# A two-layer graph network: the adjacency's own pipeline moved eight steps forward, its last row block by DMA transposes

## What is computed

```python
q, k, v = x @ Wq.T + bq, x @ Wk.T + bk, x @ Wv.T + bv
a = q @ k.T / sqrt(D) + adj + adj            # 4096 x 4096
x1 = layernorm(x + softmax(a) @ v)
h = relu(adj @ (x1 @ W1) + b1)               # y = x1 @ W1
out = layernorm(x1 + adj @ (h @ W2) + b2)
```

## Time and profile before

| | |
|---|---|
| median of 3 runs | 1905.79 us |
| the profiled execution, whole | 1905.41 us |
| its span, first to last instruction | 1903.6 us |
| TensorE busy | 1896.3 us |
| VectorE busy | 1085.0 us |
| ScalarE busy | 861.9 us |
| POOL busy | 115.9 us |
| DMA, mean over the span | 244 GB/s |
| chain that ended last | TensorE 99% |

### The profile page before, as it was taken

How to read it: one execution, slowest core, us unless ns; L and a number is a source line. 1 busy time by engine, 2 the same in 40 slices (tenths; PEclk the granted TensorE clock), 3 DMA queues, 4 the chain that set the end, 5 groups by cost and what they waited for, 6 DMA issues and landing times.

```text
span 1903.6 us, 26546 instructions
## 1 busy us (share of the span) xinstructions
PE 1896.3 (100%) x9265; PEld 889.0 (47%) x9265; DVE 1085.0 (57%) x2107; ACT 861.9 (45%) x1848; POOL 115.9 (6%) x211
## 2 busy tenths in 40 slices
PE   9999999999999999999999999999999999999998
PEld 4444444444444444444444444444444454444446
DVE  7787666666666666666666666666666620001334
ACT  6655554555555555555555555455545611010112
POOL 0000000000000000000000000000000000002334
PEclk9999999999999999999999999999999999999999
DMA  8664599999999999999999999999999999989996
GB/s 253 164 140 113 134 232 230 225 231 225 223 225 227 225 230 232 222 229 220 230 228 226 228 226 226 229 223 225 228 218 240 215 354 387 387 301 360 394 394 243
DMA packets 801015, 463.73 MB, mean 244 GB/s; under 512 B 646768, under 2 KB 654704, under 8 KB 800880
## 3 DMA queue, kind: packets, MB, share of 16 engines
q1 hardware_dynamic: 792816, 448.03, 93.7%
q10 hardware_dynamic: 8064, 14.00, 2.0%
HBM read 220.99 MB, written 92.01 MB: 164 GB/s over the span
## 4 chain that ended last, share of the span: by engine, by line
PE 99%; DMA 0%; issue 0%; DVE 0%; ACT 0%; SPq 0%; POOL 0%; POOLq 0%; ACTq 0%
PE bank L597 15%; PE bank L599 15%; PE bank L598 15%; PE bank L719 12%; PE bank L721 12%; PE bank L720 12%; PE bank L842 5%; PE bank L844 5%; PE bank L843 5%; PE bank L625 1%; PE bank L806 0%; PE bank L802 0%; PE bank L803 0%; PE bank L863 0%; PE bank L865 0%; PE bank L864 0%
## 5 line engine op out<-in xcount | busy, mean ns | idle before, releaser
L1013 ACT ACTIVATE tsp<-ring,sc 128x512 f16<-128x512 f32 x248 | 179.0, 722 | 599.0 <-DMA tsp<-tsp 598.3
L1399 DVE SCALAR_TENSOR_TENSOR ring<-bank,sc,adj_in 128x512 f32<-128x512 f32 x256 | 192.2, 751 | 398.2 <-PE bank L599 392.9
L597 PE MATMUL bank<-xT,gT 128*128 128x512 f16 x1024 | 388.1, 379 | 0.0
L598 PE MATMUL bank<-xT,gT 128*128 128x512 f16 x1024 | 388.1, 379 | 0.0
L599 PE MATMUL bank<-xT,gT 128*128 128x512 f16 x1024 | 388.1, 379 | 0.0
L719 PE MATMUL bank<-xv,tsp 128*128 128x512 f16 x1008 | 382.0, 379 | 0.1
L720 PE MATMUL bank<-xv,tsp 128*128 128x512 f16 x1008 | 382.0, 379 | 0.0
L721 PE MATMUL bank<-xv,tsp 128*128 128x512 f16 x1008 | 382.0, 379 | 0.0
L1214 DVE SCALAR_TENSOR_TENSOR tsp<-adj_in,s_a,tsp 128x512 f16<-128x512 f32 x248 | 184.7, 745 | 46.3 <-ACT tsp L1021 45.8
L1214 DVE SCALAR_TENSOR_TENSOR tsp<-ring,sc,tsp 128x512 f16<-128x512 f32 x248 | 184.9, 746 | 0.1
L1001 ACT ACTIVATE ring<-ring,bias 128x512 f32<-128x512 f32 x256 | 181.0, 707 | 8.8 <-DVE bias L1416 8.8
(11 more groups left out here) (270 smaller groups left out, 2173.3 us busy)
## 6 DMA issues: line engine op xcount, KB each, us to landing
adj_in<-in_adj SPq DMA_DIRECT2D x256, 256.0 KB, 3.2
at_dram<-tsp SPq DMA_DIRECT2D x248, 256.0 KB, 3.2
xv<-at_dram SPq DMA_DIRECT2D x54, 1024.0 KB, 14.4
adj_in<-at_dram SPq DMA_DIRECT2D x29, 1024.0 KB, 14.4
xT<-at_dram SPq DMA_DIRECT2D x20, 1024.0 KB, 14.0
xv<-in_x SPq DMA_DIRECT2D x8, 1024.0 KB, 10.0
g_dram<-tsp SPq DMA_DIRECT2D x32, 256.0 KB, 4.0
gT<-g_dram SPq DMA_DIRECT2D x32, 256.0 KB, 3.6
```

Of the source, the lines that this page charges most:

```text
L597: pe.matmul(dst, ah, bh, start=first, stop=False)
L598: pe.matmul(dst, ah, bl, start=False, stop=False)
L1013: act.activation(p_split(e)[:, 0:BANK], p, ACT.Copy, scale=col[f"p_up{batch(TW * kb)}"]).then_inc(a_p, 1)
L1399: dve.scalar_tensor_tensor(t, s_bank[s % S_BANKS][:, :], col[f"k_l{batch(s // KB)}{batch(TW * (s % KB))}"], adj_in[:, s % AR, :], ALU.mult ...
```

## The change

The adjacency's own pipeline gets its own step number. adj_plan gives for each score step s the adjacency steps that are made in it: at first v = s; in eight steps from s = 19 on, each seven after the last, two of them; from then on v = s + 8. SP, ScalarE, VectorE and POOL run load_adj, absolute_sums, adj_sum, the all-reduce, adj_scale, adj_hi, adj_lo, transpose_adj and store_at by v. So the last row block's adjacency goes through the same DMA transposes and stores as all others and is in at_dram when the scores end. TensorE's adj_transposes and the conversions after them go. The first eight units are loaded whole, 1 MB each, in an order of their own: units 0 to 3 stand between the transposes of blocks 250 to 254, units 8 and 9 stand ahead of 6 and 7. T(e) stands below for the transposes of score block e (transpose_p). Left out below are the hunks that drop the names at_bank, p_adj, the call of adj_transposes and last_adj_lo, and that call adj_plan.

```diff
@@ -88,7 +88,7 @@
 O_AT = (4, 7, 10, 13)
 STATS_DELAY, NORM_DELAY, STORE_DELAY = 1, 5, 6
 Y_LAST = (11, 14)
-ADJ_AT = (1, 2, 4, 5, 7, 8, 10, 11)
+ADJ_EARLY, ADJ_FROM = 8, 2 * KB
 Y_DRAM = NT - 4


@@ -107,6 +107,19 @@


     return list(range(t + XG + 2, t + 2 * XG + 2)) if t % XG == XG - 2 and t < NT - XG - 2 else []
+
+
+def adj_plan():
+
+
+    plan, early = [], 0
+    for s in range(NS + 2 * KB):
+        steps = [s + early]
+        if s >= ADJ_FROM and early < ADJ_EARLY and (s + early) % KB == STATS_AT - 1:
+            early += 1
+            steps.append(s + early)
+        plan.append(steps)
+    return plan


 def unit_plan():
...
@@ -472,19 +485,18 @@
                 else:
                     sp.wait_ge(p_pv, NS)
                     for i in range(2):
-                        sp.wait_ge(d_ast[i], 16 * TAIL // 2)
-                last = TAIL - KB + kb
+                        sp.wait_ge(d_ast[i], 16 * NS // 2)
+                last = TAIL + kb
                 sp.wait_ge(d_ast[last % 2], 16 * (last // 2 + 1))
-                sp.dma_start(slots[kb][:, 0:TW - 1, :, :].rearrange("p r b n -> p r (b n)"), units_dram[LAST, kb][:, 0:TW - 1, :]
-                             ).then_inc(d_unit[kb], 16)
+                sp.dma_start(slots[kb].rearrange("p r b n -> p r (b n)"), units_dram[LAST, kb]).then_inc(d_unit[kb], 16)

             def load_unit(l):
                 ic, kb, slot, after = loads[l]
                 if after:
                     sp.wait_ge(p_unit, after)
                 elif slot < KB + 3:
-                    sp.wait_ge(p_adj, min(3 + 4 * (slot - KB), KB))
-                    sp.wait_ge(v_al, TAIL)
+                    sp.wait_ge(v_add, NS)
+                    sp.wait_ge(v_al, NS)
                     if slot == KB + 2:
                         sp.wait_ge(p_pv, NS)
                 else:
@@ -516,23 +528,23 @@
                     transpose_p(TAIL - 1)
                     transpose_x1(NT - 3)
                     transpose_p(TAIL)
-                a = s - ADJ_LAG
-                if 0 < a <= NS:
-                    store_at(a - 1)
-                if 0 <= a < TAIL:
-                    transpose_adj(a)
                 if s == 4:
                     store_g(NT // XG - 1)
                     for q in (10, 11):
                         load_adj(q)
-                if 9 < s + AHEAD < NS and s + AHEAD >= 12:
-                    q = s + AHEAD
-                    if q == AR - 1:
-                        sp.wait_ge(a_w1, 1)
-                        sp.wait_ge(v_w1, 1)
-                    if q >= AR:
-                        sp.wait_ge(v_al, q - AR + 1)
-                    load_adj(q)
+                for v in adj_steps[s]:
+                    a, q = v - ADJ_LAG, v + AHEAD
+                    if 0 < a <= NS:
+                        store_at(a - 1)
+                    if 0 <= a < NS:
+                        transpose_adj(a)
+                    if 12 <= q < NS:
+                        if q == AR - 1:
+                            sp.wait_ge(a_w1, 1)
+                            sp.wait_ge(v_w1, 1)
+                        if q >= AR:
+                            sp.wait_ge(v_al, q - AR + 1)
+                        load_adj(q)
                 if NS - Y_EARLY <= s + 1 < NS:
                     load_y(s + 1 - (NS - Y_EARLY))
                 if kb == GT_AT and 1 <= r < NT - 1:
@@ -550,24 +562,23 @@
                         sp.wait_ge(v_y, j + 1)
                         sp.dma_start(y_dram[j], y_st[:, j % 2, :, :].rearrange("p two f -> p (two f)")).then_inc(d_y[j % 2], 16)

-            for i in range(KB):
-                if i:
-                    transpose_p(TAIL + i)
-                if i == 1:
-                    store_at(TAIL - 1)
-                if i == 3:
-                    load_first_unit(0)
-                if i == 5:
-                    store_x1(NT - 2)
-            load_first_unit(1)
-            load_first_unit(2)
+            transpose_p(TAIL + 1)
+            store_at(NS - 1)
+            for i in range(2, 6):
+                transpose_p(TAIL + i)
+                load_first_unit(i - 2)
+            store_x1(NT - 2)
+            for i in range(6, KB):
+                transpose_p(TAIL + i)
+            load_first_unit(4)
             sp.wait_ge(p_x1, 1)
             sp.wait_ge(d_x1, 16 * (NT - 1))
             sp.dma_start(xr[:, :], x[P * (NT - 1):P * NT, :]).then_inc(d_xr, 16)
-            for kb in range(3, KB):
-                load_first_unit(kb)
+            load_first_unit(5)
             for l in range(KB, KB + 2):
                 load_unit(l)
+            for kb in range(6, KB):
+                load_first_unit(kb)
             store_x1(NT - 1)

             sp.dma_start(w2_s, w2[:, :]).then_inc(d_late, 16)
@@ -756,17 +767,6 @@
                     last = pe.transpose(ht_bank[c % 2][:, P * j:P * (j + 1)], hs[c % 2][:, P * j:P * (j + 1)], ident)
                 last.then_inc(p_h, 1)

-            def adj_transposes(kb):
-                if kb == 0:
-                    pe.wait_ge(g_id, 4)
-                    pe.wait_ge(v_add, NS)
-                if kb >= 2:
-                    pe.wait_ge(v_al, TAIL + kb - 1)
-                for j in range(TW):
-                    last = pe.transpose(at_bank[kb % 2][:, P * j:P * (j + 1)],
-                                        adj_in[:, (TAIL + kb) % AR, P * j:P * (j + 1)], ident)
-                last.then_inc(p_adj, 1)
-
             for s in range(NS + LAG):
                 r, kb = divmod(s, KB)
                 if s < NS:
...
@@ -822,8 +820,6 @@
                 slot = loads[load][2]
                 if half == 0:
                     pe.wait_ge(d_unit[slot], 16 * (sum(1 for l in loads[:load + 1] if l[2] == slot) + (slot < Y_DRAM // TW)))
-                    if n == 0:
-                        pe.wait_ge(v_al, TAIL + kb + 1)
                     if conv == 1 and k == 0:
                         pe.wait_ge(a_h, i + 1)
                         pe.wait_ge(v_h, i + 1)
@@ -1020,15 +1016,6 @@
                     act.wait_ge(d_at[a % 2], 16 * (a // 2))
                 act.activation(asp[a % 2][:, 0:BANK], adj_in[:, a % AR, :], ACT.Copy, scale=s_a[:, r:r + 1]).then_inc(a_ah, 1)

-            def last_adj_hi(kb):
-                if kb == 0:
-                    act.wait_ge(v_sa, NT)
-                act.wait_ge(p_adj, kb + 1)
-                if kb == 6:
-                    act.wait_ge(v_al, TAIL)
-                act.activation(slots[kb][:, TW - 1, 0:TW, :], at_bank[kb % 2][:, :].rearrange("p (b n) -> p b n", n=P), ACT.Copy,
-                               scale=s_a[:, NT - 1:NT]).then_inc(a_ah, 1)
-
             def x1_hi(r):
                 act.wait_ge(v_x1, r + 1)
                 if r >= 1:
@@ -1062,25 +1049,20 @@
                 e = s - EXP_LAG
                 if 0 <= e < NS:
                     exponentials(e)
-                if s + 1 < NS:
-                    absolute_sums(s + 1)
-                a = s - ADJ_LAG
-                if 0 <= a < TAIL:
-                    adj_hi(a)
+                for v in adj_steps[s]:
+                    if v + 1 < NS:
+                        absolute_sums(v + 1)
+                    if 0 <= v - ADJ_LAG < NS:
+                        adj_hi(v - ADJ_LAG)
                 if s >= 2 * KB and kb == X1_AT:
                     x1_hi(r - 2)
                 if s >= 3 * KB and kb == YOUT_AT:
                     y_hi(r - 3)
             for i in range(KB):
                 exponentials(TAIL + i)
-                if i % 2:
-                    last_adj_hi(i // 2)
-                if i == 3:
+                if i == 6:
                     y_hi(NT - 3)
-                if i == 7:
-                    last_x1_hi(NT - 2)
-            for kb in range(KB // 2, KB):
-                last_adj_hi(kb)
+            last_x1_hi(NT - 2)
             y_hi(NT - 2)
             last_x1_hi(NT - 1)

...
@@ -1496,12 +1473,13 @@
                     row_max(s)
                     if kb == KB - 1:
                         exp_bias(r)
-                        adj_sum(r)
-                if kb == 0 and 1 <= r <= NT:
-                    adj_scale(r - 1)
-                a = s - ADJ_LAG
-                if 0 <= a < TAIL:
-                    adj_lo(a)
+                for v in adj_steps[s]:
+                    if v % KB == KB - 1 and v < NS:
+                        adj_sum(v // KB)
+                    if v % KB == 0 and KB <= v <= NS:
+                        adj_scale(v // KB - 1)
+                    if 0 <= v - ADJ_LAG < NS:
+                        adj_lo(v - ADJ_LAG)
                 if s >= 2 * KB:
                     if kb == STATS_AT:
                         attention_rows(r - 2)
@@ -1514,17 +1492,13 @@
             p_lo(TAIL - 1)
             for i in range(KB):
                 p_lo(TAIL + i)
-                if i % 2:
-                    last_adj_lo(i // 2)
-                if i == 3:
+                if i == 4:
                     attention_rows(NT - 2)
+                if i == 5:
```

(23 more changed lines are left out.)

6 lines of the change are left out of this document (removed).

## The result

The changed kernel takes 1925.14 us (median of four runs, 1922.41 to 1926.85) where the kernel before takes 1905.68: 1.0101 times as long, interval 1.0083 to 1.0118. It is slower by 19.5 us. The prediction was 1909.3, in a range up to 1912.3. The profiled execution took 1925.05 us, with a span of 1923.2 against 1903.6.

A forecast was written before the change was run, and what follows sets the result against it. TensorE's own instruction list was taken as the bound. Handover waits of 5.9 less 3.5 removed gave +2.5, plus 0.9 for a pause, rounded to +3.5 on the median 1905.79: 1909.3 us, range 1904.9 to 1912.3.

The forecast's parts named there:

- the score stage: Eight double adjacency steps, score steps 19 to 68: SP's lateness is recovered from its waits; cost nothing, bounds 0 and +2 us.
- Rival D: Score stage: double steps hold up TensorE, 2 us over the forecast, 1911.3 us; chance 0.06.
- The removed work: Eight groups of 4 TensorE transposes between 1508.6 and 1539.8 us go, all on the path: -3.5 us.
- The handover: From 1505 to 1540 us, transposes wait behind units: waits 5.9, gain 3.5, +2.5 us; with the pause +3.5.
- the pause: Handover: the DMA queue stands nearly still among the new loads; bounds 0 and 1.7 us, 0.9 taken.
- A: Handover: units don't hold up the transposes, so the unit stream decides, -0.3 to +1.4, about 1906.3 us; chance 0.22.
- C: Handover: every turn from a transpose to a unit costs extra, +6.1, 1911.9 us; chance 0.22.
- B: The whole gain arrives, 1902.3 us, if the queue finds the 2 to 4 us it lacks; chance 0.06.
- The unit stream: Second stage: last unit lands 2.2 to 3.9 us later with 2.5 to spare; -0.3 to +1.4 us without handover waits.

The follow-up runs named there:

- e1: Changed kernel with its eight double steps 15 or more score steps apart instead of 7; 1912.63 us, 1.0040 times the kernel before.
- e10: Changed kernel with its eight double steps still 7 apart, but from step 163 on instead of step 19; 1927.21 us, 1.0113 times the kernel before.
- e2: Changed kernel with ScalarE doing the adjacency's sums and high half ahead of the exponentials in each step; 1918.98 us, 1.0069 times the kernel before.
- e3: Changed kernel with the loads of units 0 to 3 behind the last transposes instead of between them; 1920.64 us, 1.0078 times the kernel before.
- e4: Changed kernel with the edits of e2 and e3 together; 1913.56 us, 1.0041 times the kernel before.
- e6: Changed kernel with the edits of e1 and e3 together; 1909.56 us, 1.0022 times the kernel before.
- e7: e1 with the first eight units loaded without their fourth row block (0.75 MB), leaving part of a product wrong; 1909.91 us, 1.0024 times the kernel before.
- e5: e1 with the first two units issued at score steps 251 and 253, the rest behind later transposes; 1907.43 us, 1.0011 times the kernel before.

## Why the prediction was wrong

**The step that failed: the score stage, costed at nothing with a bound of +2; it was +13.0.** The double step's own lateness was right (3.6 to 4.5 forecast, 4.7 measured for block 10), and so was SP's order of work. The next sentence was wrong: SP's waits, 152 us in 1240, were taken as time that a late SP gets back, 4.5 us in seven steps. It got back 1.6 (4.7 to 3.1 and 6.3 to 4.7). The free time was overrated too: the prediction had 4.6 us at worst, while block 46 in the kernel before landed at 460.17 and was used at 463.63, 3.5 us later. The waits are not idle time with a deadline behind it. They end when VectorE has done the work of a step that itself began with a landing of SP's own transposes, or when SP's own transposes land (3.1 us at least). Move SP by 4 us and the end of these waits moves too. e1 shows the accumulation, e10 that only the spacing counts, e2 that the loop through ScalarE is about half of it; for the other half, the landings of SP's own transposes, the rise of that wait (3.3 to 14.7 us) is what the traces show, and no run removed it. The bound of 2 us came from one double step against TensorE's slack; with a recovery of 1.6 for each 4 to 5 lost, eight had to be added up. Rival D named the place and the mechanism, but priced it at 2 us and gave it 0.06.

**The removed work: right.** 3.5 us off TensorE's list; e3, e4 and e6 show it as -3.3, -3.2 and -3.2.

**The handover: right in kind, 2.6 us too low.** Forecast +3.5 net, measured +6.1. The waits themselves came to 6.2, not the 6.8 of the sum (5.9 and 0.9 for the pause); what is on top of them are 3.4 of clock: behind each of the two waits TensorE ran at 1.2 GHz for seven or eight matmuls, a term that the sum did not have. The pause was 1.5 us, not 0.9, near its upper bound of 1.7. Against that, the forecast 0.6 and 1.0 before blocks 252 and 253 did not come up, since waiting 2.3 instead of 1.6 before 251 and the slow clock had already moved TensorE behind these landings. That 6.2 lies so near 6.8 is in part luck: errors of both signs cancel.

On the rule of the Trainium skill, "Advanced Engine Details and Errata", section "X-Bar Transpose (TRN2)", that transposes are as fast as regular DMAs: T(254) and T(255), in line, landed at 1551.82 and 1552.76, 0.94 apart. That is the 0.9 of the rows, and not the 0.68 that the prediction took for a plain copy of that size; e1's x1 store, such a copy, landed 0.69 behind u3. Behind a unit or the store it is less: T(252), T(253) and T(254) landed 0.82, 0.80 and 0.75 us after what stood ahead of them. So the rule is off in this trace, and the 0.9 was somewhat high for three of the four; either way it is under 0.9 us of the sum.

**The rivals.** A (units don't hold up transposes) is out: landings of 6.4 to 8.0 us behind units, 3.1 to 3.3 without (e3). C (a price for each turn) is out by e7, and by the changed kernel itself, where T(251) to T(253) landed 3.58 us apart against 3.6 for a unit and a transpose. D was right in kind, at more than six times its price. B would have needed e3, e5 or e6 to end below before; none does. The unit stream's own estimate, -0.3 to +1.4 when the handover is free of waits, holds at its edge: e3 and e6 give +1.5. The last unit landed 3.8 us later against the end of the score stage in e3 (2.2 to 3.9 forecast), though TensorE paid for it earlier, at the xr load and at units 6 and 7.

**Left open.** Where the pause comes from. In the changed kernel it falls together with a packet of instruction fetch on another DMA queue, at 1549.0 us, between u3 and x1's store; e1 and e7 have it one DMA later, ahead of T(254), and again with such a packet (1536.3 and 1534.4 us). The traces narrow it down. In e3, e4 and e6 the same packet comes (1544.8, 1537.0, 1531.9 us) when the last transposes have landed and only loads are in flight, and nothing stops. The stretch behind the packet in the changed kernel, then in e3 (the last number is GB/s):

```profile
1549.40:1550.90 1.50, 0.00 (x0) 0.00 (x0) 0.00 (x0) 0.00 (x0) 0.00 (x0) 1.00 1.35 26
```

```profile
1544.80:1546.30 1.50, 1.50 (x9) 0.68 (x8) 0.00 (x0) 0.00 (x0) 0.00 (x0) 1.00 1.01 385
```

So the packet alone does not do it: in the handover the pause was seen only with transposes in flight, and why is not shown. Also open is why the changed kernels scatter by 1 to 6 us between runs (lowest to highest) and the kernel before by 0.7 to 1.9; the clock, below, may be a part of it, which is argued and not shown. How far e5 stands from the kernel before is just above what can be measured (interval from 1.0001).

## What to carry to other kernels

A queue's waits are spare only when what ends them does not depend on that queue; before you spend them, follow each back to what released it, and if the way leads through the queue's own earlier DMAs, add lateness up over all the moved steps. Spread extra work farther apart than the time in which its lateness dies out (here 15 steps left 0.0 to 1.4 us, and 7 steps 13 or more). And when a queue that lands in order is as full as its consumer is, removing 3.5 us of compute by adding 2 MB of loads in front of it gains little: 0.4 us at best here.

## What the hardware showed that I had not expected

**One wait can bring the slow clock.** After waits of 2.27 us (391.20), 2.10 (431.43) and 2.12 (1538.13), TensorE went from 2.4 to 1.2 GHz for seven to nine matmuls, 0.43 us between starts instead of 0.216, about 1.7 us each time. In e2 and e10, before block 254, the clock fell while TensorE still waited (3.8 us) and stayed low for about twelve matmuls, 2.6 us. It isn't the length of the wait alone: in e1 a wait of 3.8 us before block 254 was followed by no slow matmul, and the window from 1520 to 1560 us has a clock of 1.00 there and 0.91 in the changed kernel:

```profile
1520.00:1560.00 40.00, 33.18 (x173) 15.59 (x172) 8.02 (x26) 2.19 (x4) 0.55 (x1) 1.00 1.09 345
```

TensorE's waits from 1490 us on in e1, then e7; e7's, the shorter, brought eight slow matmuls:

```profile
PE bank L730 <- DMA adj_in<-tsp: 3.8, 1, 3.8
...
PE bank L731 <- DMA adj_in<-tsp: 3.2, 1, 3.2
```

In all traces here, from 20 to 1880 us, 13 of TensorE's 18 waits of 2.05 to 3.97 us came with slow matmuls, and none of those of 1.04 to 1.97 us did. So waits of 2 us and more need a term of their own in a sum: nothing, 1.7 or 2.6 us.

**SP's issue can slow down when much is outstanding.** A transpose that takes 1.24 to 1.3 us to issue took 2.97 and 3.47 (T(253) and T(255), rows of the handover above), with one or two units and other DMAs not yet landed, and that is a delay for what stands behind it. T(254), with u3 and others in flight, took 1.39, so what decides is not shown.
